# Moving the first batch's output projection, norm and gate logits into the ring of maxima, and the value projection in front of the attention

## The reference

```python
q = (x @ Wq.T + bq).reshape(B, T, H, D)          # k, v likewise
scores = jnp.einsum('bqhd,bkhd->bhqk', q, k) * attn_scale[0]
scores = jnp.where(mask[None, None], -jnp.inf, scores)
attn = jax.nn.softmax(scores, axis=-1)
out = jnp.einsum('bhqk,bkhd->bqhd', attn, v).reshape(B, T, C) @ Wo.T + bo
x = layernorm(x + out)
s = sigmoid(x @ gate_weight.T)                    # groups, then the six best, normed, times 2.5
routed = sum over e of combine[:, e] * ((silu(x @ g_e.T) * (x @ u_e.T)) @ d_e.T)
x = layernorm(x + routed + shared)
```

## Time and profile before

| | us |
|---|---|
| median of three runs | 478.77 |
| the three runs | 480.24, 478.51, 478.77 |
| the profiled execution, its own time | 480.55 |
| its span, first to last instruction | 478.5 |
| TensorE busy / VectorE / ACT / GpSimd | 421.6 / 365.3 / 219.8 / 112.1 |
| mean granted clock of TensorE | 0.911 |

### The profile page before, as it was taken

How to read it: one execution, slowest core, us unless ns; L and a number is a source line. 1 busy time by engine, 2 the same in 40 slices (tenths; PEclk the granted TensorE clock), 3 DMA queues, 4 the chain that set the end, 5 groups by cost and what they waited for, 6 DMA issues and landing times.

```text
span 478.5 us, 8023 instructions
## 1 busy us (share of the span) xinstructions
PE 421.6 (88%) x2864; PEld 221.3 (46%) x2864; DVE 365.3 (76%) x810; ACT 219.8 (46%) x291; POOL 112.1 (23%) x190
## 2 busy tenths in 40 slices
PE   5329959999999999999999875799999999999992
PEld 1015522433333343434333443477766666666660
DVE  4818897999999999999993637458678958855863
ACT  4500026686777677685866632222234232323220
POOL 5000040535546363535251440000000000000000
PEclk9855558999999999999999975699999999999998
DMA  4542340011020202020000000373223342442330
GB/s 116 172 178 94 118 121 21 4 51 56 31 74 21 84 6 97 9 75 17 3 4 3 2 0 0 85 126 99 98 76 102 108 124 89 143 143 88 115 106 23
DMA packets 27039, 34.50 MB, mean 72 GB/s; under 512 B 5560, under 2 KB 16120, under 8 KB 27000
## 3 DMA queue, kind: packets, MB, share of 16 engines
q1 hardware_dynamic: 26686, 33.34, 23.1%
q10 hardware_dynamic: 314, 0.66, 0.4%
HBM read 29.33 MB, written 4.65 MB: 71 GB/s over the span
## 4 chain that ended last, share of the span: by engine, by line
PE 63%; DVE 19%; SPq 8%; DMA 3%; issue 3%; ACT 2%; POOL 1%; DVEq 0%; POOLq 0%; ACTq 0%
PE ps L1245 12%; PE ps L1147 11%; DVE mx L818 10%; PE ps L1104 9%; PE ps L1215 7%; PE ps L1217 7%; PE ps L1216 6%; PE ps L1128 5%; SPq L490 3%; SPq L544 3%; PE ps L1108 2%; PE ps L1168 1%; DMA scratch<-mh 1%; DVE oT L803 1%; DVE oT L799 1%
## 5 line engine op out<-in xcount | busy, mean ns | idle before, releaser
L818 DVE TENSOR_REDUCE mx<-ps 128x1 f32<-128x512 f32 (+3 forms) x304 | 180.4, 652 | 24.8 <-PE ps L1108 17.6
L725 ACT ACTIVATE probs<-ps 128x1024 f32<-128x1024 f32 (+2 forms) x160 | 143.2, 941 | 66.8 <-PE ps L1128 66.4
L1104 PE MATMUL ps<-rows_k,rows_q 48*128 48x512 bf16 (+3 forms) x384 | 98.8, 359 | 21.6 <-DMA rows_k<-scratch 14.5
L785 ACT ACTIVATE sg<-ps 128x512 f32<-128x512 f32 x68 | 40.8, 600 | 100.7 <-PE ps L1217 99.5
L1147 PE MATMUL ps<-probs,Vg 128*32 128x512 f32 (+3 forms) x768 | 83.6, 510 | 0.0
L1128 PE MATMUL ps<-rows_q,rows_k 51*128 51x512 bf16 (+3 forms) x384 | 76.3, 334 | 5.4 <-DMA rows_q<-scratch 5.1
L1215 PE MATMUL ps<-x1hi,w_hi 128*128 128x512 f32 x136 | 75.9, 558 | 0.9 <-ACT probs L725 0.9
L1045 DVE TENSOR_TENSOR au<-ps,sg 128x512 f32<-128x512 f32 x64 | 44.1, 689 | 39.4 <-PE ps L1245 37.0
L1104 PEld LDWEIGHTS ps<-rows_k,rows_q 48*128 48x128 bf16 x384 | 29.0, 95 | 93.3 <-DVE mx L818 62.6
L1245 PE MATMUL ps<-hh,w_down 128*128 128x512 f32 x136 | 69.7, 595 | 0.8 <-DVE hh L1050 0.8
L642 POOL TENSOR_SCALAR_AFFINE_SELECT probs<-probs 64x512 f32<-64x512 f32 x64 | 42.2, 659 | 106.1 <-ACT probs L725 104.9
(11 more groups left out here) (102 smaller groups left out, 336.2 us busy)
## 6 DMA issues: line engine op xcount, KB each, us to landing
comb_rows<-weights SPq DMA_DIRECT2D x128, 128.0 KB, 2.9
scratch<-oT SPq DMA_DIRECT2D x8, 384.0 KB, 3.6
w_raw<-in_unitT SPq DMA_DIRECT2D x17, 128.0 KB, 6.0
rows_q<-scratch SPq DMA_DIRECT2D x16, 96.0 KB
rows_k<-scratch SPq DMA_DIRECT2D x14, 96.0 KB
w_down<-in_unitT SPq DMA_DIRECT2D x1, 1088.0 KB, 6.6
xT<-in_xT SPq DMA_DIRECT2D x4, 256.0 KB, 4.2
rows_q<-scratch SPq DMA_DIRECT2D x16, 64.0 KB
```

Source lines behind the costliest of these rows:

```text
L725: act.activation(dst, src, ACT.Exp).then_inc(exps_ready, 1)
L818: dve.tensor_reduce(dst, src, AX.X, ALU.max).then_inc(max_read, 1)
L1104: mm = pe.matmul(bank(max_bank(k), m, at), q, rows_k[r0:r0 + ROWS_QK, s, j * T + k0:j * T + k0 + m], start=True, stop=not first, tile_posi ...
```

## The change

1. Batch 0's sixteen steps up to the second "logit" become entries of the ring of maxima, ahead of the units of `TAIL_UNITS`, counted from unit 216 (group 5's 27th). Each takes the next of the three banks. VectorE's pieces without a bank (`SMALL_JOBS`: gate split, statistics, moments, norm) stand behind given units. The router follows the last "top" at once, and the two "comb" steps are the ring's last entries, planned among group 7's exponentials. A "comb" is copied and stored by ACT between exponentials.
2. The value tiles are projected behind the query and key projections, two each, which now use banks 6 and 7; `wv` is loaded earlier and has its own semaphore.
3. ACT issues its six row loads of group 0 ahead of its last two projections. SP waits for all rows of group 0 before it stores the last four parts. The rows of group 2 are loaded between the first two stores of maxima, `w_down` behind the second. `bob` is loaded before `wo`.
4. SP no longer waits for the exponentials of group 5 before it serves the gate weights of the experts.
5. The limit of the lead counts transposed maxima (`TOPS_THROUGH`), not entries. `masks_before` becomes 40 and 48 (it was 57 and 61): the roots follow the last mask of group 4 and of group 5.

```diff
+TAIL_FROM = 5 * 38 + 26
+TAIL_UNITS = [0, 3, 6, 9, 13, 17, 19, 22, 25, 28, 32, 35, 38, 41, 52, 55]
+SMALL_JOBS = {-3: ("gate", 0), 18: ("stats", 0), 20: ("moments", 0), 30: ("norm", 0), 39: ("stats", 1),
+              42: ("moments", 1), 50: ("norm", 1)}
...
+                if units_so_far in steps:
+                    entries.append(("tail", steps[units_so_far], None, None, None))
...
+    return entries + waiting + [("tail", k, None, None, None) for k in range(COMB, len(TAIL))]
...
-        if k / (NM + 2) - i["e"] / NE > LEAD and i["e"] < len(ev):
+        if TOPS_THROUGH[k] / 2 - i["e"] / NE > LEAD and i["e"] < len(ev):
...
-            which = k % 2 if b == 0 else 1
-            return tail_read[which], bank(6 + which)
+            if b == 0:
+                return tail_read[k % 2], bank(max_bank(TAIL_ENTRY[k]))
+            return tail_read[1], bank(BACK)
...
+            sp.wait_ge(rows_loaded[0], ROWS_ALL)
+            for n in range(NC, 2 * NC):
+                store_parts(n)
             sp.wait_ge(slots_cleared, 2 * (NS - 1))
-            for g in range(1, NS):
-                load_rows(g)
+            load_rows(1)
...
-            sp.dma_start(w_down[:, :, :], a["unitT"][:, :, 2 * P:3 * P]).then_inc(downs_loaded, 16)
             for g in range(NG):
                 store_max(g, 0)
+                if g == 0:
+                    load_rows(2)
                 store_max(g, 1)
+                if g == 0:
+                    sp.dma_start(w_down[:, :, :], a["unitT"][:, :, 2 * P:3 * P]).then_inc(downs_loaded, 16)
...
-            sp.wait_ge(exp_scores, NE * (NG - 2))
...
             for n in range(2 * NC):
+                if n == 6:
+                    act.wait_ge(parts_stored[0], 16 * NC)
+                    act.wait_ge(slot0_cleared, 2)
+                    load_row_tensor(act, 0, 1)
...
+            for k in range(len(ENTRIES)):
+                if ENTRIES[k][0] == "unit":
+                    reduce(k)
+                elif ENTRIES[k][0] == "top":
+                    split_top(k)
+                else:
+                    early_step(ENTRIES[k][1])
+                if k in JOB_AFTER:
+                    small_job(*JOB_AFTER[k])
+                if k == LAST_TOP:
+                    for n in range(ROUTER_SLICES):
+                        router(0, n)
...
-                pe.matmul(bank(n % 2), (wq, wk)[n % 2][:, :], xT[:, n4 * BANK:(n4 + 1) * BANK],
+                pe.matmul(bank(PROJ_BANK + n % 2), (wq, wk)[n % 2][:, :], xT[:, n4 * BANK:(n4 + 1) * BANK],
                           start=True, stop=True).then_inc(proj_done, 1)
...
+                if n == 1:
+                    pe.wait_ge(wv_loaded, 16)
+                if n >= 1:
+                    project_values(2 * n - 2)
+                    project_values(2 * n - 1)
```

208 lines of the change are left out of this document (123 added, 85 removed).

## The result

The median of four runs of the changed kernel is 474.06 us (472.28 to 474.43); the kernel before, on the same chip, took 479.39 (478.51 to 480.24). The ratio is 0.9882 (95% interval 0.9848 to 0.9915), so the change is faster clear of noise, by 5.3 us between the medians, where 18.9 were forecast. The profiled execution took 474.43 with a span of 472.5.

What follows compares the result with a forecast made beforehand. VectorE was taken to bound the ring of maxima until 252 us, TensorE the experts from 309.56. 9.5 (E) - 18.4 (D) + 27.8 (F) = 18.9 us off the median of 478.77: about 460, range 451 to 470.

Steps and rivals of the forecast that it cites:

- E: Start of the kernel: the ring of maxima runs 9.5 us earlier (5 to 11.5).
- I had given them 1.0: Projections at the start: two value tiles behind each delay batch 0's parts by 1.0 us, bounds 0 and 11.5.
- the rows are there at about 26.3: Start: group 0's rows land at about 26.3 instead of 32.8, moving the first reduction from 33.66 to 28.7.
- SP's wait behind x: Start, before the maxima's store: SP waits 12.13 us at the load after x, reaching the store at about 53.
- what GpSimd's addition takes back: Start, second split: GpSimd's bias addition to x slows VectorE beside it, costing 1.5 us (0 to 4).
- D: Ring of maxima: it lasts 18.4 us longer (14.4 to 25) with batch 0's sixteen steps inside.
- first term: Ring of maxima: the moved steps add 14.4 us of VectorE work, while TensorE's steps (about 12 us) run beside it.
- The two waits that I did price: Ring of maxima: VectorE waits for ScalarE's copies, 1.5 us together; GpSimd's first root delays a mask, 2.5 us (0 to 5).
- F: From the last transposed maxima to the steady experts: this stretch shrinks by 27.8 us (22 to 29).
- the 8 us of TensorE's work "at the upper level": Between the last exponential and the steady experts: TensorE needs 8 us at the upper clock level, plus a 0.6 us copy.
- The router was hidden: Behind the ring: the 10.7 us router is done 12 us after the last maxima, hidden beside the exponentials.
- Rival 5: Ring of maxima: clock falls when TensorE waits for VectorE's added jobs, and stays; 24 us more, 484; chance 0.04.

Runs made afterwards that it cites:

- both_useless: Kernel before with the changed start, plus useless VectorE additions and useless TensorE transposes and matmuls at the moved steps' places: 488.94 us, ratio 1.0191.
- nudged: Changed kernel plus two useless fp32 TensorE matmuls ahead of each of units 296, 298 and 300: 467.66 us, ratio 0.9776.
- vector_only: Kernel before with the changed start, plus useless VectorE additions alone at the moved steps' places: 484.24 us, ratio 1.0098.

## Why the prediction was right, and where it failed

**E was right in size (9.8 for 9.5), its steps only in part, so the size is partly luck.** The value tiles cost the parts nothing: SP's row loads start at 18.39 against 18.34 before; I had given them 1.0. The step that failed is "the rows are there at about 26.3": they landed at 31.95. With no stores beside them the loads of rows were still in flight until then, so the reduction moved by 0.9 us, not 5. Two errors on the other side made up for it: VectorE ran group 0 without a gap (18.8 us from first reduction to split, for 21), and SP's wait behind x was 6.61 us instead of 12.13. The store at 51.59 (forecast 53), its 2 us and the first exponential scores at 57.20 (forecast 57.5) were right. So was what GpSimd's addition takes back: VectorE's cast and subtraction beside it last 1.00 and 0.83 us, some 1.3 more than the same two of the first split, for 1.5 forecast.

**D failed in its first term.** It puts the 14.4 us "all on the bounding engine" and lets TensorE's steps "run beside it", as "It has room: 69 of 72 us before": that costed TensorE's steps at nothing. VectorE's own work was near enough (15.0 us for 14.4). The three useless-work kernels put VectorE's work alone at 14.8 us, TensorE's alone at 14.1 and both at 19.5. TensorE, busy 96% of the stage, was a second bound here, and adding to both cost more than the larger. The two waits that I did price, ScalarE's copy (1.4 us in all, 1.5 forecast) and GpSimd's root, were there; the latter was mis-sized, some 0.6 us for 2.5. Beyond the 19.1 us of both_useless, whose own ring has the clock low for 6.8 us, stand 6.3: 1.4 for the copy, 0.6 for the root and 2.2 for the clock's fall at 259. The other 2.1 lie between the low stretch at 225 and the waits of the steps, and no run parts them.

**F failed in the 8 us of TensorE's work "at the upper level".** The fall at 259 outlasts the ring, to 276.4, and the clock is low again at 290.1 and 300.3: nudged, whose clock behind the ring is low for 3.4 us instead of 15.9, has a rest 3.7 us shorter (201.5 to 205.2). ScalarE's table load and the SiLU behind the last copy weren't in the sum; they are 1.7 us more. 21.6 + 3.7 + 1.7 = 27.0, close to the 27.8 forecast. The router was hidden and the comb rows waited for nobody, as forecast; the last exponential was 1.5 us late (23.0 for 21.5; 20.5 in nudged).

**The rivals.** Rival 5 had the clock falling inside the ring, and its mechanism (TensorE waits for VectorE's added jobs) shows in vector_only at 198.8. In the changed kernel the fall at 225.2 stands right behind the logits (223.65 to 225.16), and that at 259.3 where TensorE, with exponentials dry, waits 1.35 us for VectorE's reductions, none of them an added job. The price was wrong: the clock came back after 13.7 and 17.1 us, and the fall at 259.3 cost 5 to 6 us, not 24. It should have stood as a term of every case, not as a case of 0.04 on its own. The Trainium skill, "TensorE: Matmul & The Clock Gate" (Part 4), says of transposes that they do not count as TensorE's activity in the same way. No run here parts them from other short work, and the fall at 259.3 has only one transpose in the 3 us before it, at 256.66.

## What to carry to other kernels

An engine at 96% beside the bounding one had no room here. To cost work that is moved into a full loop, put useless work of the same size there on each engine alone and on both, before the real dependences. A gain of a few per cent from an edit that moves hardly any row may be the clock's; compare the granted clock of the stages, and of single executions, before believing the edit's own story. And an edit's cover has to be asked for the clock too: where a stream of matmuls runs dry just ahead of a stretch that depends on one engine, both stretches pay.
